# Two graph layers fused in one loop: announced jumps back, moved reads and copies, and a new order of small steps on VectorE

## The chip, the cores and the metric

One core of a Trainium2 chip runs the whole program. The metric is the device time of one execution in microseconds (us), lower is better. The engines are TensorE (PE, with its weight loads PEld), VectorE (DVE), ScalarE (ACT), GpSimd (POOL) and SyncE (SP); a small q behind a name (DVEq) is that engine's sequencer, which reads registers, waits for semaphores and issues.

## The reference, cut to what matters

There are 6250 nodes with 256 features and 206250 edges, sorted by target node. Layer 1 sums, over a node's edges, the neighbour's features beside 64 edge features, multiplies by a message matrix, and passes the result through a layer norm, a three-layer perceptron and a second norm. Layer 2 computes for every edge a logit from 128 other edge features, and for every node a softmax over its edges of the neighbours' hidden rows.

```python
agg = segment_sum(concat(x[src], edge64) @ W_message, dst)
h = layer_norm(relu(agg) + x); x1 = layernorm(x + layer_norm(x + mlp(h)))      # layer 1
edge_h = lrelu(edge128 @ ew_W + ew_b); hid = lrelu(x1 @ w_W + w_b)              # layer 2
e = concat(hid[tgt], hid[nbr], edge_h) @ a_W + a_b
out = lrelu(segment_sum(softmax_over_tgt(e) * hid[nbr], tgt)); y = layernorm(x1 + out)
```

## The kernel before, in words

A preparing stage counts edges by block of 128 nodes and writes small tables. Then comes the fused stage, the subject here, and behind it the second gather stage, which lies from about 2985 us of the span to the end and which the diff does not touch.

The fused stage is one loop of 51 passes, written out on each engine by itself (`Fori` on SP, POOL, PE, ACT and DVE); the engines keep in step by counting semaphores alone. A pass p holds 32 positions kk, and on PE, ACT and DVE a hand-written order puts small steps of three jobs at these positions:

- **Edge logits.** At every kk PE multiplies one tile of 128 edges (`edge` on PE, L657) into one of five PSUM banks that ACT filled with the bias before (`seed`, L801, three positions ahead), and DVE reduces it to one logit column (`edge` on DVE, L1034). Banks go round, so a seed waits until DVE has read the bank's last tile, and PE waits for the seed. SP loads the edge features four tiles at a time into two halves (`feats`, L600).
- **Sorting the logits.** The logits of pass p-1 are split into three bf16 parts (`split_logits`, L1014 to L1019, five instructions), multiplied by a one-hot of the target's block (`tag_logits`, L1024, at kk 0 to 2), and `sort` on PE (L696, from kk 4) puts them in order. `tag_keys` (L1006) does the same to the keys, `slots` (L995) makes the one-hot of the places, `key_pairs` (L999) doubles the keys, `place` (L1030) copies the addresses at which POOL writes the sorted rows (L617).
- **Layer 1.** POOL gathers the neighbours' rows, 35 indirect DMAs a pass (`gathers`, L624), from indices that `pick` (L1041, eight a pass) copied out. `one_hot` (L1060) on DVE and `add_rows` on PE (L672) sum them into one bank, `take_sums` (L1068, kk 30) takes the sum, and a chain of node steps turns the block before into its result: on DVE `add_x` at 5, `first_norm` 7, `residual` 12, 15 and 18, `out_sum` 21, `out_norm` 23, `last_norm` 25 (L1128), `table` 30 (L1134 to L1140); on PE the matmuls between them (L731 for the perceptron, `turn_x1` at 28, `hidden` at 30, L751); on ACT the copies, and `take_p` at 31 (L848), which waits for the table.

Each engine carries out its own order in sequence; a wait holds everything behind it on that engine. On DVE a step that needs the result of the step just before waits for it with `wait_alone` (L111 to L114). `edges_at` (L565) and `tile_at` (L562) read a pass's numbers from a table in SBUF into registers; on DVE both stand at the head of the pass, before `split_logits`:

```python
with dve.Fori(0, n) as p:
    e = edges_at(dve, p)
    tile = tile_at(dve, p + 1)
    body(p, e, tile)
```

On SP a pass begins with `load_x`, which waits for `last_norm` of the pass before (L591), and the two reads; only then come the loads of the edge features.

Of the kernel before, what the change touches and what calls it, by code (L numbers as in the profile page):

```python
# [27 lines left out]
P = 128  # L28
# [30 lines left out]
def build(nc, a, n_nodes, n_edges):  # L59
# [24 lines left out]
    with ExitStack() as top:  # L84
# [30 lines left out]

# [341 lines left out]
        with ExitStack() as ctx:  # L458
# [108 lines left out]
            @block.sync  # L567
            def _(sp):
                def load(dst, src):
                    sp.dma_start(dst, src).then_inc(w_in, 16)  # L570

                load(w_edge[:, 0:D], a["ew_W"])
                for n, name in enumerate(("a_tgt", "a_nbr", "a_edge")):
                    load(row[name], a["a_W"][n:n + 1, :].to_broadcast([P, D]))
                for name in ("w_b", "ew_b", "aggr_scale", "aggr_bias", "out_scale", "out_bias"):
                    load(row[name], a[name].to_broadcast([P, D]))
                load(ab_col[:], a["a_b"].to_broadcast([P, 1]))
                for c in range(KC):
                    load(w_msg[:, c, :], a["W_message"][c * P:(c + 1) * P, :])
                    load(w_node[:, c, :], a["w_W"][c * P:(c + 1) * P, :])  # L580
                    for n in range(3):
                        load(w_mlp[:, n, c, :], a[f"mlp_W{n}"][c * P:(c + 1) * P, :])
                load(w_msg[0:DE0, KC, :], a["W_message"][D:D + DE0, :])
                for n in range(3):
                    load(b_mlp[:, n, :], a[f"mlp_b{n}"])

                def load_x(p):

                    sp.wait_ge(nx["x1"], p)
                    d = block_at(sp, p)  # L590
                    sp.dma_start(x_blk[:], a["x"][bass.ds(d * P, P), :]).then_inc(nx["x"], 16)  # L591

                n = count_of(sp)
                with sp.Fori(0, n) as p:
                    load_x(p)
                    e = edges_at(sp, p)
                    t0 = tile_at(sp, p)
                    for c in range(TILES // EB):
                        sp.wait_ge(o["y_ready"], p * TILES + (c * EB - EB + Y0))
                        sp.dma_start(feats[:, c % 2 * EB * P:(c % 2 + 1) * EB * P],  # L600
                                     a["edge128"][:, bass.ds(e * (TILES * P) + c * EB * P, EB * P)]).then_inc(f_in[c % 2], 16)
                        j, at = c, STARTS[c]
                        sp.wait_ge(o["summed"], p * NB_SUMS + (j + 1))
                        sp.dma_start(rows[:, at:at + SUMS[j], D:W0], a["edge64"][:, bass.ds(t0 + at, SUMS[j]), :]).then_inc(e_in[j], 16)
                load_x(n)
                wait_alone(sp, (nx["tab_out"], n * 16 + 16))
# [4 lines left out]
            def _(pool):  # L611
# [20 lines left out]
                with pool.Fori(0, n) as p:  # L632
# [11 lines left out]
            def _(pe):  # L644
# [130 lines left out]
                with pe.Fori(0, n) as p:  # L775
                    body(p)
# [14 lines left out]
            def _(act):  # L791
# [11 lines left out]
                def keep_triangle(p):  # L803
                    act.wait_ge(o["tri_ready"], p + 1)
                    act.wait_ge(o["turned"], p * U + 1)
                    s.copy(starts[:].rearrange("p u b -> p (u b)"), TRI).then_inc(o["tri_kept"], 1)

# [52 lines left out]
                def body(p):  # L860
                    for kk in range(TILES):
                        seed(p, kk + AHEAD)
                        if kk in (8, 16):
                            pack(p, (8, 16).index(kk))
# [10 lines left out]
                for kk in range(AHEAD):  # L875
                    seed(0, kk)
                n = count_of(act)
                with act.Fori(0, n) as p:
                    body(p)
                steps = [node[kk] for kk in sorted(node)]  # L880
# [14 lines left out]
            def _(dve):  # L895
# [102 lines left out]
                def key_pairs(p, at):  # L998
                    v.tensor_copy(key_two[:], key[:, :, bass.ds(at, TILES)].unsqueeze(3).to_broadcast([P, 3, TILES, 2])  # L999
                                  ).then_inc(o["keys_ready"], 1)  # L1000

# [26 lines left out]
                def place(w, u, e):  # L1028
                    dve.wait_ge(rows_out, w * (U * 16) + (u + 1) * 16)
                    v.tensor_copy(at_now[u][:], at_all[:, bass.ds(e * U + u, 1)]).then_inc(o["at_ready"], 1)  # L1030

# [4 lines left out]

                def pick(p, j, tile):

                    if not isinstance(p, int):
                        dve.wait_ge(o["summed"], p * NB_SUMS + (j + 1))  # L1040
                    v.tensor_copy(picked[j][:, 0:SUMS[j]], src_i[:, bass.ds(tile + STARTS[j], SUMS[j])]).then_inc(o["picked_ready"], 1)  # L1041
# [104 lines left out]
                pick_at = {(SUM_KK[j + 1] + 1 if j + 1 < NB_SUMS else TILES - 1): j for j in range(NB_SUMS)}  # L1146
                hot_at = {SUM_KK[j - 2] + 1: j for j in range(2, NB_SUMS)}

                def body(p, e, tile):
                    at = e * TILES  # L1150
                    split_logits(p, at)
                    for kk in range(TILES):
                        edge(p, kk)
                        if kk < 3:
                            tag_logits(p, kk)
                        if kk == 3:
                            find(p, at)
# [6 lines left out]
                        if kk in (9, 13):  # L1164
                            place(p, (9, 13).index(kk), e)
                        if kk == 10:
                            key_pairs(p, at)
# [10 lines left out]
                        if kk in (18, 21, 23, 27):  # L1178
                            slots(p, (18, 21, 23, 27).index(kk))
                        if kk in (19, 25, 29):  # L1180
                            tag_keys(p, (19, 25, 29).index(kk))
                        if kk in hot_at:
                            one_hot(p, hot_at[kk])
                        if kk in pick_at:
                            pick(p + 1, pick_at[kk], tile)
                        if kk in node:
                            node[kk](p)
                        if kk == 24:
                            base_of(p + 1)
# [15 lines left out]
                for u in range(U):  # L1205
                    v.tensor_copy(at_now[u][:], dump[:]).then_inc(o["at_ready"], 1)
                tile = tile_at(dve, 0)
                for j in range(NB_SUMS):
                    pick(0, j, tile)
# [3 lines left out]
                one_hot(0, 1)  # L1213
                n = count_of(dve)
                with dve.Fori(0, n) as p:
                    e = edges_at(dve, p)
                    tile = tile_at(dve, p + 1)
                    count[0] = 0
                    body(p, e, tile)
                e = edges_at(dve, n)  # L1220
                split_logits(n, e * TILES)
                for m in range(3):
                    tag_logits(n, m)
                for u in range(U):
                    place(n, u, e)
# [608 lines left out]
```

## Time and profile before

| what | value |
|---|---|
| median of 3 runs | 5291.64 us (5288.85 to 5291.9) |
| the profiled execution, its own time | 5291.46 us |
| its span | 5289.7 us |
| fused stage, 48 passes in step | about 319 to 2777 us of the span |
| mean granted TensorE clock | 0.892 |

The profile is one execution; its busy shares are means over stages with different limits. A row of waits counts idle time of an engine and names what ended it. Times in timelines count from the start of the span.

### The profile page before, as it was taken

Reading aid. Unit: us, or ns where it says so; the run is one execution under the profiler, and the core shown is the slowest. Engines: PE = TensorE matmul, PEld = TensorE weight load, DVE = VectorE, ACT = ScalarE, POOL = GpSimd, SP = SyncE. Lnnn points to the kernel's source line nnn. Section 1 sums busy time; section 2 is a strip of 40 time slices with the busy share of each in tenths; the row PEclk is TensorE's granted clock in tenths of the full one; section 3 lists DMA queues with packets and bytes.
Section 4 is the critical chain, followed back from the end, with each engine's and each line's share of the span. In section 5 each row is a group of like instructions: output and inputs, shape, how many; then the busy total and the mean of one; then the engine's idle time right before and its main releaser. Section 6 shows DMA issues by size and latency. Waiting matters only on the chain. (4 is left out here: it accounts for less than half of the span.)

```text
span 5289.7 us, 86818 instructions
## 1 busy us (share of the span) xinstructions
PE 3902.5 (74%) x18662; PEld 2967.3 (56%) x18663; DVE 3563.6 (67%) x11443; ACT 1726.2 (33%) x5121; POOL 3584.2 (68%) x3655
## 2 busy tenths in 40 slices
PE   4498989898989898988887366666666666666661
PEld 3366666666666666666665255555555555555551
DVE  8778888888888888888786455555555555555554
ACT  0133333232323333333332133333333333333334
POOL 0377776777777777777773277777777777777772
PEclk9799999999999999999998688888888888888886
DMA  1356555555555555555556334344444334433343
GB/s 44 96 164 170 158 164 154 165 155 161 157 162 157 160 157 160 157 162 160 157 164 94 101 107 106 106 106 106 106 106 106 106 106 105 107 106 106 106 105 64
DMA packets 544286, 679.76 MB, mean 129 GB/s; under 512 B 340246, under 2 KB 376430, under 8 KB 543996
## 3 DMA queue, kind: packets, MB, share of 16 engines
q0 software_dynamic: 174144, 469.02, 32.6%
q1 hardware_dynamic: 355132, 196.63, 13.8%
q10 hardware_dynamic: 14976, 13.69, 0.8%
q8 instruction: 18, 0.29, 0.0%
q14 instruction: 16, 0.13, 0.0%
HBM read 650.32 MB, written 27.79 MB: 128 GB/s over the span
## 5 line engine op out<-in xcount | busy, mean ns | idle before, releaser
L624 POOL DMA_INDIRECT rows<-in_x,picked x1785 | 1799.1, 1008 | 724.1 <-issue 686.0
L1499 POOL DMA_INDIRECT room<-nodetab,nbr_idx x1736 | 1643.8, 947 | 562.4 <-issue 490.2
L672 PE MATMUL bank<-rows,hot 128*128 128x320 f32 x3570 | 1237.5, 446 | 25.7 <-DMA rows<-in_edge 19.7
L657 PE MATMUL bank<-w_edge,feats 128*128 128x258 f32 x3264 | 1050.6, 411 | 213.0 <-DMA feats<-in_edge 108.7
L801 ACT COPY bank<-b_edge 128x258 f32<-128x258 f32 x1635 | 602.7, 377 | 1460.6 <-DVE unused L1034 1442.9
L1529 PE MATMUL bank<-room,w 128*128 128x258 f32 x3472 | 1037.9, 462 | 51.2 <-ACT w L1575 50.7
L1561 ACT ACTIVATE w<-off,logit 128x128 f32<-128x128 bf16 x1736 | 534.0, 388 | 1361.0 <-DVE logit L1613 1361.0
L1529 PEld LDWEIGHTS bank<-room,w 128*128 128x128 f32 x3472 | 802.8, 238 | 244.4 <-ACT w L1575 95.0
L1520 PE MATMUL bank<-ident,w 128*128 128x128 f32 x1736 | 307.4, 330 | 777.2 <-ACT w L1561 777.2
L657 PEld LDWEIGHTS bank<-w_edge,feats 128*128 128x128 f32 x3264 | 578.7, 200 | 433.3 <-ACT bank L801 197.6
L1034 DVE SCALAR_TENSOR_TENSOR unused<-bank,a_relu 128x258 bf16<-128x258 f32 x1632 | 687.5, 421 | 199.2 <-PE bank L657 173.6
L672 PEld LDWEIGHTS bank<-rows,hot 128*128 128x128 f32 x3570 | 704.7, 198 | 179.9 <-issue 41.9
L1520 PEld LDWEIGHTS bank<-ident,w 128*128 128x128 f32 x1736 | 233.3, 166 | 824.0 <-ACT w L1561 437.0
L1618 DVE TENSOR_REDUCE best<-bank 128x1 f32<-128x896 f32 x248 | 270.7, 1091 | 475.0 <-PE bank L1520 474.9
L1613 DVE TENSOR_TENSOR logit<-r_at,room 128x7 f32<-128x7 f32 x248 | 42.4, 171 | 455.4 <-DMA room<-nodetab,nbr_idx 454.6
L1608 DVE TENSOR_SCALAR off<-iota_bf,lane_f 128x128 bf16<-128x128 bf16 x1736 | 337.8, 276 | 1.6 <-issue 1.6
L696 PE MATMUL bank<-tagged,slot 128*128 128x300 bf16 x1664 | 283.5, 293 | 54.9 <-DVE tagged L1024 54.6
L1637 DVE TENSOR_TENSOR w<-w,bank 128x896 f32<-128x896 f32 x248 | 268.5, 1083 | 58.2 <-PE bank L1512 55.3
L1060 DVE TENSOR_TENSOR hot<-iota,rel 128x512 f32<-128x512 f32 (+1 forms) x410 | 300.8, 734 | 0.1
L696 PEld LDWEIGHTS bank<-tagged,slot 128*128 128x128 bf16 x1664 | 159.4, 98 | 198.6 <-issue 143.0
L1575 ACT ACTIVATE w<-w 128x896 f32<-128x896 f32 x248 | 231.7, 934 | 4.4 <-DVE w L1637 4.4
L617 POOL DMA_INDIRECT recs<-out_rows,at_now x106 | 107.3, 1012 | 111.9 <-ACT out_rows L815 80.9
(316 smaller groups left out, 3871.4 us busy)
## 6 DMA issues: line engine op xcount, KB each, us to landing
feats<-in_edge SPq DMA_DIRECT2D x408, 256.0 KB, 2.9
rows<-in_edge SPq DMA_DIRECT2D x255, 128.0 KB, 3.0
rows<-in_x,picked POOLq DMA_INDIRECT x1785, 2.9
room<-nodetab,nbr_idx POOLq DMA_INDIRECT x1736
rows<-in_edge SPq DMA_DIRECT2D x153, 160.0 KB, 3.4
nodetab<-tab ACTq DMA_DIRECT2D x52, 129.0 KB, 2.7
x_blk<-in_x SPq DMA_DIRECT2D x52, 128.0 KB, 2.1
x_rows<-u_n ACTq DMA_DIRECT2D x52, 128.0 KB, 2.3
```

The lines of the kernel that those rows point to most:

```text
L624: pool.indirect_dma_start(out=rows[:, STARTS[j] + s, 0:D], out_offset=None, in_=a["x"], in_offset=bass.IndirectOffsetOnAxis(ap=picked[j][: ...
L657: mm(y, feats[:, f0 * P:(f0 + 1) * P], w_edge[:], start=False, stop=True, skip_group_check=True).then_inc(o["y_ready"], 1)
L672: ins = mm(S_PS, hot[j % HR][:, s - STARTS[j], :], rows[:, s, :], start=(s == 0), stop=(s == SA - 1), skip_group_check=True)
L696: ins = mm(SORT, slot[:, at, :], tagged[:, at, :, :, :].rearrange("p n f b -> p (n f b)"), start=(t == 0), stop=(t == L - 1), skip_group_c ...
L801: s.copy(logits_of(kk), b_edge[:]).then_inc(o["seeded"], 1)
L1034: v.scalar_tensor_tensor(unused[:, kk % EB, :], logits_of(kk), 0.0, a_relu[:], ALU.max, ALU.mult, accum_out=r_cur[:, kk:kk + 1]).then_inc( ...
L1060: v.tensor_tensor(hot[j % HR][:, 0:SUMS[j], :], iota[:].unsqueeze(1).to_broadcast(shape), rel[:, at:at + SUMS[j]].unsqueeze(2).to_broadcas ...
L1499: pool.indirect_dma_start(out=nbr[:, u * GC + k, :], out_offset=None, in_=nodetab, in_offset=bass.IndirectOffsetOnAxis(ap=nbr_idx[u][:, k: ...
L1520: ins = nc.tensor.transpose(T_PS[u % 2][:, k * P:(k + 1) * P], w[:, u * GC + k, :], ident[:])
L1529: ins = mm(O_PS[u % 2][:, 0:HW], w[:, u * GC + k, :], nbr[:, u * GC + k, :], start=(k == 0), stop=(k == GC - 1))
L1561: ins = s.activation(w[:, u * GC + k, :], off[:, u * GC + k, :], ACT.Identity, bias=logit[u][:, k:k + 1])
L1608: v.tensor_scalar(off[:, u * GC + k, :], iota_bf[:], lane_f[:, bass.ds(tile0(i, u) + k, 1)], MASKED, ALU.not_equal, ALU.mult)
```

## The change

On DVE `split_logits` moves from the head of a pass to the end of the pass before, `edges_at` is read at kk 0 and `tile_at` at kk 18. `place`, `key_pairs` and `pick` (eleven copies a pass) go from DVE to ACT, with reads of the same numbers there at kk 3 and 5. The steps `tag_keys`, `slots`, `base_of`, `local` and `one_hot` of the next pass get other positions.

```diff
+        def passes_of(eng, start, end):
+            return nc.Fori(start, end, engines=bass.OrderedEngineSet([eng.engine]), hint_back_edge=True)
...
-                with sp.Fori(0, n) as p:
-                    load_x(p)
+                with passes_of(sp, 0, n) as p:
...
+                        if c == 0:
+                            load_x(p)
...
                     for kk in range(TILES):        # ACT
                         seed(p, kk + AHEAD)
+                        if kk == 3:
+                            e = edges_at(act, p)
+                        if kk == 5:
+                            tile = tile_at(act, p + 1)
+                        if kk in (9, 13):
+                            place(p, (9, 13).index(kk), e)
+                        if kk == 6:
+                            key_pairs(p, e)
+                        if kk in pick_at:
+                            pick(p + 1, pick_at[kk], tile)
...
+                for u in range(U):                 # ACT, before its loop, after its first three seeds
+                    s.copy(at_now[u][:], dump[:]).then_inc(o["at_ready"], 1)
+                tile = tile_at(act, 0)
+                for j in range(NB_SUMS):
+                    pick(0, j, tile)
...
-                def body(p, e, tile):              # DVE
-                    at = e * TILES
-                    split_logits(p, at)
+                def body(p):
                     for kk in range(TILES):
                         edge(p, kk)
                         if kk < 3:
                             tag_logits(p, kk)
+                        if kk == 0:
+                            at = edges_at(dve, p) * TILES
+                        if kk == 18:
+                            tile = tile_at(dve, p + 1)
...
-                        if kk in (9, 13):
-                            place(p, (9, 13).index(kk), e)
-                        if kk == 10:
-                            key_pairs(p, at)
...
-                        if kk in (18, 21, 23, 27):
-                            slots(p, (18, 21, 23, 27).index(kk))
-                        if kk in (19, 25, 29):
-                            tag_keys(p, (19, 25, 29).index(kk))
+                        if kk in (18, 21, 26, 28):
+                            slots(p, (18, 21, 26, 28).index(kk))
+                        if kk in (17, 20, 25):
+                            tag_keys(p, (17, 20, 25).index(kk))
...
-                        if kk in pick_at:
-                            pick(p + 1, pick_at[kk], tile)
...
-                        if kk == 24:
+                        if kk == 22:
                             base_of(p + 1)
                             go_on(p)
-                        if kk == 25:
+                        if kk == 23:
                             local(p + 1, tile)
-                        if kk == 26:
+                        if kk == 24:
                             one_hot(p + 1, 0)
-                        if kk == 28:
+                        if kk == 27:
                             one_hot(p + 1, 1)
                         if kk == 30:
                             take_sums(p)
+                    split_logits(p + 1, at + TILES)
```

## Rows read from the trace of the kernel before

**Rows 1.** The page: busy us of each engine, its share of the span, instructions.

```profile
PE 3902.5 (74%) x18662; PEld 2967.3 (56%) x18663; DVE 3563.6 (67%) x11443; ACT 1726.2 (33%) x5121; POOL 3584.2 (68%) x3655
```

**Rows 2.** Windows: length, busy us of PE, PEld, DVE, ACT, POOL, clock, DMA share, GB/s.

```profile
319.20:2778.00 2458.80, 2213.65 (x10203) 1613.60 (x10202) 1986.86 (x6914) 758.36 (x2303) 1769.29 (x1756) 0.96 0.56 160
```

**Rows 3.** Waits in the same stretch: waiter, releaser, us in total, times, longest.

```profile
POOL rows L624 <- issue: 645.0, 1609, 4.0
...
PE bank L657 <- ACT bank L801: 101.3, 137, 2.1
PE bank L657 <- DMA feats<-in_edge: 91.6, 47, 3.0
...
DVE r_rest L1014 <- issue: 88.8, 48, 2.0
...
PE bank L696 <- DVE tagged L1024: 51.2, 42, 1.9
...
DVE h_t L1109 <- PE bank L731: 18.3, 47, 0.4
```

**Rows 4.** DVE's first step of a pass, L1014: ns min/median/max, first and last start.

```profile
L1014 DVE TENSOR_TENSOR r_rest<-r_cur x48: 191/193/194, 319.2 to 2777.2; 128x32 f32<-128x32 f32 x48
```

**Rows 5.** Timeline of one pass, layer 2 of the perceptron and kk 25.

```profile
2022.68 0.61 DVE L1109 SCALAR_TENSOR_TENSOR h_t<-bank,b_mlp,h_t 128x128 f32<-128x128 f32 x2 [0.39 <-PE bank L731]
...
2033.14 0.99 DVE L1006 TENSOR_TENSOR tagged<-hb,key_two 128x1600 bf16<-128x1600 bf16 x1
...
2034.04 0.16 DVE L1041 COPY picked<-src_i 128x4 int32 x1
...
2034.11 0.16 DVE L1085 RECIPROCAL rstd<-std 128x1 f32<-128x1 f32 x1
```

**Rows 6.** Timeline of the same pass's end and the next one's head.

```profile
2034.36 0.41 DVE L1128 TENSOR_SCALAR u_n<-u,mv,rstd 128x256 f32<-128x256 f32 x1
...
2037.54 1.12 PE L751 MATMUL bank<-w_node,h_t 128*128 128x256 f32 x4
...
2040.04 0.41 DVE L1134 TENSOR_TENSOR u<-bank,row_w_b 128x256 f32<-128x256 f32 x1
...
2042.97 0.29 ACT L848 ACTIVATE p_all<-p_cur,ab_col 128x1 f32 x1 [3.69 <-DVE stats L1140]
...
2043.80 2.09 PE L657 MATMUL bank<-w_edge,feats 128*128 128x258 f32 x4 [1.83 <-ACT bank L801]
...
2045.34 0.19 DVE L1014 TENSOR_TENSOR r_rest<-r_cur 128x32 f32<-128x32 f32 x1 [1.85 <-issue]
...
2046.21 0.43 DVE L1034 SCALAR_TENSOR_TENSOR unused<-bank,a_relu 128x258 bf16<-128x258 f32 x1 [0.19 <-DVE r_two L1019]
...
2050.28 0.68 PE L696 MATMUL bank<-tagged,slot 128*128 128x300 bf16 x4 [0.39 <-DVE tagged L1024]
```

**Rows 7.** DVE's jump and table read by line, 300 to 2800 us.

```profile
L1215 DVEq COMPARE_BRANCH  x48: 56/56/56, 316.9 to 2774.9; - x48
L1215 DVEq FUSED_REGOPS  x48: 74/74/74, 317.2 to 2775.2; - x48
...
L565 DVEq TENSOR_LOAD <-pass_tab x48: 521/531/689, 317.3 to 2775.3; - x48
```

**Rows 8.** DMA queues in 300 to 2800 us, all of them: packets, MB, share.

```profile
q0 software_dynamic: 85520, 225.99, 31.1%
q1 hardware_dynamic: 282056, 161.27, 23.9%
q10 hardware_dynamic: 13824, 12.64, 1.5%
```

**Rows 9.** The edge matmuls of the whole span, by line.

```profile
L657 PE MATMUL bank<-w_edge,feats x3264: 378/381/802, 207.4 to 2905.0; 128*128 128x258 f32 x192
```

**Rows 10.** Timeline of the start of the fused stage.

```profile
203.76 1.07 DVE L1041 COPY picked<-src_i 128x5 int32 x8 [0.84 <-issue]
...
206.62 1.67 ACT L801 COPY bank<-b_edge 128x258 f32<-128x258 f32 x5 [2.65 <-issue]
...
214.86 2.50 PE L672 MATMUL bank<-rows,hot 128*128 128x320 f32 x4 [5.49 <-DMA rows<-in_x,picked]
```

More of the change, by code:

```diff
@@ L631, in _ @@
                 n = count_of(pool)
-                with pool.Fori(0, n) as p:
+                with passes_of(pool, 0, n) as p:
                     gathers(p, 0)
@@ L774, in _ @@
                 n = count_of(pe)
-                with pe.Fori(0, n) as p:
+                with passes_of(pe, 0, n) as p:
                     body(p)
@@ L806, in keep_triangle, with place, key_pairs, pick @@
                     s.copy(starts[:].rearrange("p u b -> p (u b)"), TRI).then_inc(o["tri_kept"], 1)
+                def place(w, u, e):
+                    act.wait_ge(rows_out, w * (U * 16) + (u + 1) * 16)
+                    s.copy(at_now[u][:], at_all[:, bass.ds(e * U + u, 1)]).then_inc(o["at_ready"], 1)
+                def key_pairs(p, e):
+                    act.wait_ge(o["tagged_ready"], p + 1)
+                    s.copy(key_two[:], key[:, :, bass.ds(e * TILES, TILES)].unsqueeze(3).to_broadcast([P, 3, TILES, 2])
+                           ).then_inc(o["keys_ready"], 1)
+                def pick(p, j, tile):
+                    if not isinstance(p, int):
+                        act.wait_ge(o["summed"], p * NB_SUMS + (j + 1))
+                    s.copy(picked[j][:, 0:SUMS[j]], src_i[:, bass.ds(tile + STARTS[j], SUMS[j])]).then_inc(o["picked_ready"], 1)
+                SUM_KK = [SUM_AT[at] for at in STARTS]
+                pick_at = {(SUM_KK[j + 1] + 2 if j + 1 < NB_SUMS else TILES - 1): j for j in range(NB_SUMS)}
                 def pack(w, u):
@@ L876, in _ @@
                     seed(0, kk)
+                for u in range(U):
[3 more added lines that the diff above has]
+                    pick(0, j, tile)
                 n = count_of(act)
-                with act.Fori(0, n) as p:
+                with passes_of(act, 0, n) as p:
                     body(p)
+                e = edges_at(act, n)
+                for u in range(U):
+                    place(n, u, e)
                 steps = [node[kk] for kk in sorted(node)]
@@ L996, in slots @@
                                     ALU.is_equal).then_inc(o["slot_ready"], 1)
-                def key_pairs(p, at):
-                    v.tensor_copy(key_two[:], key[:, :, bass.ds(at, TILES)].unsqueeze(3).to_broadcast([P, 3, TILES, 2])
-                                  ).then_inc(o["keys_ready"], 1)
                 def tag_keys(p, n):
@@ L1026, in tag_logits @@
                         ins.then_inc(o["tagged_ready"], 1)
-                def place(w, u, e):
-                    dve.wait_ge(rows_out, w * (U * 16) + (u + 1) * 16)
-                    v.tensor_copy(at_now[u][:], at_all[:, bass.ds(e * U + u, 1)]).then_inc(o["at_ready"], 1)
                 def edge(p, kk):
@@ L1035, in edge @@
                                            accum_out=r_cur[:, kk:kk + 1]).then_inc(o["logit_ready"], 1)
[L1037 to L1041, printed above, removed]
                 def base_of(p):
@@ L1145, in _ @@
                 SUM_KK = [SUM_AT[s] for s in STARTS]
-                pick_at = {(SUM_KK[j + 1] + 1 if j + 1 < NB_SUMS else TILES - 1): j for j in range(NB_SUMS)}
                 hot_at = {SUM_KK[j - 2] + 1: j for j in range(2, NB_SUMS)}
-                def body(p, e, tile):
-                    at = e * TILES
-                    split_logits(p, at)
+                def body(p):
                     for kk in range(TILES):
@@ L1204, in _ @@
                 dve.sem_inc(nx["s"], 1)
-                for u in range(U):
-                    v.tensor_copy(at_now[u][:], dump[:]).then_inc(o["at_ready"], 1)
                 tile = tile_at(dve, 0)
-                for j in range(NB_SUMS):
-                    pick(0, j, tile)
                 base_of(0)
@@ L1213, in _ @@
                 one_hot(0, 1)
+                split_logits(0, 0)
                 n = count_of(dve)
-                with dve.Fori(0, n) as p:
-                    e = edges_at(dve, p)
-                    tile = tile_at(dve, p + 1)
+                with passes_of(dve, 0, n) as p:
                     count[0] = 0
-                    body(p, e, tile)
-                e = edges_at(dve, n)
-                split_logits(n, e * TILES)
+                    body(p)
                 for m in range(3):
                     tag_logits(n, m)
-                for u in range(U):
-                    place(n, u, e)
                 count[0] = 0
```

## The prediction, made before the changed kernel was run

> **What bounds the kernel now.** I read the page first: no engine is busy for more than three quarters of the span, so averages say nothing [rows 1]. The change touches only the fused stage, so I cut that out. Its passes are steady: 47 lie between the first and the last start of DVE's first step, 2458.0 us, or 52.30 us each [rows 4]. Per pass (the busy times over 47) PE is busy 47.1, DVE 42.3, POOL 37.6, ACT 16.1 us [rows 2]. POOL needs more than it shows: it leaves about 0.30 us between two of its 37 DMAs, so 37.6 + 11.1 = 48.7 us, and has 3.6 us of room a pass (its "issue" wait is 645.0/47 = 13.7 us, mostly those 0.30s) [rows 3]. That is a floor for later.
>
> Then the waits, to see who paces whom. DVE waits 0.39 us a pass for layer 2 of the perceptron (18.3/47), idles 1.85 us at the head of its pass on "issue", and PE waits for DVE's `tagged` 1.1 us, for ACT's seeds 2.2 us, for `feats` 1.9 us [rows 3]. The timeline orders this. From 2022.68, where DVE waits 0.39 us for layer 2 [rows 5], it never waits for PE again until after the pass's end: table at 2040.04, pass head at 2045.34, first edge at 2046.21. PE in turn runs dry there (1.83 us for a seed at 2043.80, 0.39 for `tagged` at 2050.28), and from `sort` at 2050.28 it is full until it hands layer 2 back to DVE [rows 6]. So a pass is two stretches in series: **DVE's** from layer 2 (kk 18) across the pass's end to `sort`, 2022.68 to 2050.28, 27.6 us; and **PE's** from `sort` to layer 2, the other 24.7 us. What shortens the first counts; what leaves DVE in the second does not, since DVE waits there for PE anyway.
>
> **Pass numbers read in mid-pass, logits split before the jump.** Of DVE's 1.85 us, the two reads are 2 x (0.53 + about 0.4 of register work) [rows 7]. In the new order edge 31 is followed by the split after a wait of about 0.19 us (what such a wait for its own result costs, [rows 6]), 0.68 us of split instructions, then jump and register work, about 0.55 us, then edge 0. Before, from the end of edge 31 to edge 0 it was 1.85 + 0.16 for the last `pick`, + 0.87 (2045.34 to 2046.21) = 2.8 us or so; now 0.19 + 0.68 + 0.55 = 1.4 to 1.5. **Gain 1.3 us** on DVE up to `tag_logits`. The reads themselves move under cover: at kk 0 behind a 0.99 us `tagged` product, at kk 18 behind `tag_keys` (0.99) and an edge (0.42) that are already issued; a read is about 0.9 us of sequencer. I take nothing, with 0 to 0.5 each if the queue is empty.
>
> How much passes through to `sort`? PE must be there too. It waits for `tagged` in 42 of 47 passes, 1.1 us on average, from 0 to 1.9 [rows 3]. The reason for the spread is PE's clock: the granted clock of this stretch is 0.96 on average [rows 2], and the four edge matmuls at 2043.80 take 2.09 us [rows 6], where the usual one takes 0.38 and the slowest 0.80 [rows 9]. After its dry spell PE works for a while at 1.2 instead of 2.4 GHz, now longer, now shorter. Of DVE's 1.3 us PE can use at most what it waited in each pass: with waits spread from 0 to 1.9 around 1.1 that is about **1.0 us**; bounds 0.4 (the pass shown) and 1.3.
>
> **Copies moved, steps reordered.** A `pick` is 0.16 us long but overlaps: 2034.04 to the next start 2034.11 is 0.07 us [rows 5]. Four of the eight stand in DVE's stretch before the table: 0.28 us. The others, both `place` and `key_pairs` stand in PE's stretch or are counted above: nothing. `tag_keys` 0 goes from kk 19 to 17, ahead of the wait for layer 2: DVE arrives 0.9 later (2033.14 to 2034.04) where it idled 0.39 and loses a 0.07 `pick`, so it saves 0.46. All the other moved steps stay between layer 2 and the table. Sum 0.74 us. What it opens: `last_norm` now has only 3.7 us of DVE work between itself and the table (three edges less two products; before 5.3, 2034.77 to 2040.04), and PE's `hidden` ends 3.9 us after it (2037.54 + 1.12) of which some was waiting for a seed that now comes sooner [rows 6]. So a new wait of 0 to 0.3 us; I take 0.15. **Gain 0.6 us**, bounds 0.1 and 0.8. The table lets ACT's `take_p` go (2042.97), and that the seed and PE at 2043.80, so this 0.6 moves both sides of the meeting at `sort` and passes through whole.
>
> On ACT eleven copies, at 0.29 (its 128x1 instruction [rows 6]) to 0.4, and two reads: about 4.5 us beside 16.1 busy of 52.3 [rows 2]. Their waits are for things long done (`summed` two positions back). If one blocked, the seeds behind it would wait, and PE for them.
>
> **SP.** Features for edges 0 to 3 leave earlier, so PE's 1.9 us for `feats` goes [rows 3]. But edges 2 and 3 still wait for the seed that hangs on the table: the idle time moves there. Nothing.
>
> **Start.** The first indices are now copied by ACT, behind PE's priming (206.62), three seeds, two copies and a read: first index about 208.8 instead of 203.8, and PE's first sum waits for those rows (5.49 us) [rows 10]. **+5 us**, once.
>
> **The sum.** 0.6 + 1.0 - 0.1 = 1.5 us a pass, times 48 passes in step (the first and the last two are paced by other things) = 72; less 5 = 67. Against the profiled execution, 5291.46 - 67 = 5224; that run stands 0.2 us from the median, so **5225 us**, -1.3%. Its own range: with 0.4 for the head, 0.9 a pass, 43 - 5, 5253; with 0.8 and 1.3 and nothing for the announcement, 2.1 a pass, 101 - 5, 5195.
>
> **Rivals.**
> 1. *The half-clock stretch decides.* If PE's slow spell begins as late and lasts as long with less waiting around it, PE's own 6 us from 2043.80 to 2050.28 set `sort` and only the table's 0.5 or so is left, or a read is exposed: 0.5 x 48 - 5 = 19, **5272**. For it: the pass shown gives DVE only 0.39. Against: 42 of 47 passes wait for `tagged`.
> 2. *More passes through.* The slow spell disappears as the dry spell shrinks, PE is always ready first, and DVE's whole 0.74 + 1.35 + a saved jump count: 2.2 x 48 = 106, no start cost, **5186**. POOL's room of 3.6 us a pass would allow it. Against: the seed still hangs on the table, so PE still runs dry.
> 3. *Slower: the announcement fetches.* If each announced jump brings in instructions that DVE or ACT then waits for, the price is a transfer's; the nearest rows are a DVE jump without one (0.25 us) and, far off, PE's longest wait for a landing, 3.0 us [rows 3]. At 2.1 us a pass, 101, against 67 saved: +34, **5326**. It decides from 1.4 us a pass. Against: nothing is fetched now, so what would be brought in is already there.
> 4. *The change does nothing*: PE's stretch grows by what DVE's loses, because ACT's added copies hold seeds up. 5290.
>
> The Trainium skill (Runtime: NRT & Kernel Launch, Instruction fetch mechanics) says that a taken branch whose target has left the sequencer's two-page window stalls on a fetch. By that rule, if DVE's long body outgrew the window, the jump's stall would be what the announcement removes. In this trace jump and queues show no such stall, so by the trace the term is nothing; the same rule stands beside rival 3, where code is fetched anew.
>
> **Chances.** Forecast 0.50, rival 1 0.17, rival 2 0.15, rival 3 (and ACT held up for longer) 0.10, rival 4 0.08. Within 0.2% (10.6 us), about what a measurement of this kernel can tell from no change, lies only rival 4: faster 0.82, same 0.08, slower 0.10. The range that leaves 2 in 10 out runs from rival 2's side to rival 1's: 5180 to 5280.
>
> **What would show it.** Starts of `split_logits` about 50.8 us apart; the "issue" idle at L1014 gone, with some 0.2 us after edge 31; POOL's "issue" wait down by 1.5 a pass; `feats` waits on PE gone and seed waits grown; `tagged` waits shrunk to a few tenths on average; granted clock about 0.96 as before; no instruction packets in 300 to 2700 us. Instruction packets in every pass, a new gap behind L1215 or L878, or ACT waits for L672 would make me wrong.

## The result and the profile after

The changed kernel takes **5194.64 us** (median of 4 runs, 5190.34 to 5199.08), the kernel before 5290.25 us beside it (4 runs, 5285.57 to 5291.9): ratio 0.9822, 95% interval 0.981 to 0.9833. That is 96 us less where 67 were forecast. It lies inside the range of 5180 to 5280, but 30 us below the forecast of 5225 and only 9 above rival 2's 5186. The profiled span is 5196.8 us, 92.9 less than before's.

Four views answer to those of before. The page, with each engine's busy us, share and instructions (before: [rows 1]):

```profile
PE 3824.1 (74%) x18662; PEld 2950.1 (57%) x18663; DVE 3511.6 (68%) x10870; ACT 1807.9 (35%) x5694; POOL 3555.6 (68%) x3655
```

573 instructions left DVE and as many came to ACT: the copies. Windows and waits of the fused stage, columns as in [rows 2] and [rows 3]:

```profile
319.20:2684.00 2364.80, 2133.19 (x10199) 1594.31 (x10199) 1939.85 (x6392) 832.26 (x2820) 1742.32 (x1757) 0.98 0.61 166
```

```profile
POOL rows L628 <- issue: 553.6, 1530, 3.7
...
PE bank L661 <- ACT bank L805: 200.6, 94, 2.8
DVE unused L1065 <- PE bank L661: 172.0, 315, 1.1
...
PE bank L700 <- DVE tagged L1059: 31.1, 21, 1.6
DVE u L1115 <- PE bank L722: 30.3, 47, 1.8
```

DVE's first step of a pass, `split_logits`, now L1049 ([rows 4]):

```profile
L1049 DVE TENSOR_TENSOR r_rest<-r_cur x48: 192/226/256, 319.6 to 2684.8; 128x32 f32<-128x32 f32 x48
```

47 passes take 2365.2 us, 50.32 each: 2.0 less than the 52.30 of [rows 4]. Beside it, compared with before: no wait for `feats` stands in the list any more, PE's wait for seeds has grown from 2.2 to 4.3 us a pass (200.6/47), its wait for `tagged` comes 21 times instead of 42, DVE's "issue" idle before the split is gone, POOL's "issue" has gone from 13.7 to 11.8 us a pass. All of these were forecast in kind. Two were off in size: the passes were to be 50.8 us apart, and the wait for `tagged` a few tenths of a us, where it is 31.1/47 = 0.66. Not forecast is the clock, 0.98 where it was 0.96 [rows 2]. PE's busy time shrank with it, 2213.65/47 = 47.1 to 45.4 us a pass, for the same matmuls.

The timeline of one pass's end (start, duration, idle before and its releaser; compare [rows 6]):

```profile
2027.62 0.42 DVE L1159 TENSOR_TENSOR u<-bank,row_w_b 128x256 f32<-128x256 f32 x1
...
2030.54 0.29 ACT L869 ACTIVATE p_all<-p_cur,ab_col 128x1 f32 x1 [2.66 <-DVE stats L1165]
...
2031.10 0.21 DVE L1049 TENSOR_TENSOR r_rest<-r_cur 128x32 f32<-128x32 f32 x1
...
2031.44 2.03 PE L661 MATMUL bank<-w_edge,feats 128*128 128x258 f32 x4 [2.80 <-ACT bank L805]
...
2032.50 0.43 DVE L1065 SCALAR_TENSOR_TENSOR unused<-bank,a_relu 128x258 bf16<-128x258 f32 x1 [0.60 <-DVE r_two L1054]
...
2032.85 0.99 DVE L1059 TENSOR_TENSOR tagged<-hb,r_two 128x1600 bf16<-128x1600 bf16 x1
...
2036.57 0.69 PE L700 MATMUL bank<-tagged,slot 128*128 128x300 bf16 x4
```

The table still lets the seed and the edge matmuls go 3.8 us later (2027.62 to 2031.44). But DVE's split starts 3.5 us after the table where it was 5.3, the first edge 4.9 where it was 6.2, and `sort` stands 8.95 us behind the table, with no wait, where it was 10.2 and waited.

To set the runs beside each other I worked out the same three distances in every trace, as means over 44 passes from the fourth on: from PE's first `sort` matmul to DVE's layer 2 residual, from there to the table's first step, and from there to the next `sort`. They add up to the pass. The last column is how many us of a pass PE's granted clock stood at the lower of its two levels, 1.2 instead of 2.4 GHz. All are us.

| kernel | sort to layer 2 | layer 2 to table | table to sort | pass | at half clock |
|---|---|---|---|---|---|
| before | 24.68 | 17.36 | 10.25 | 52.29 | 4.58 |
| after | 25.04 | 16.27 | 9.02 | 50.33 | 2.25 |
| announcement alone | 24.68 | 17.37 | 10.27 | 52.32 | 4.50 |
| head emptied alone | 24.68 | 17.35 | 9.19 | 51.21 | 5.20 |
| after, old positions | 24.95 | 16.91 | 9.34 | 51.19 | 4.96 |
| after, copies on DVE | 25.11 | 16.33 | 9.04 | 50.49 | 2.48 |
| after, no announcement | 25.05 | 16.25 | 8.96 | 50.26 | 2.48 |
| after, blocks first | 25.04 | 16.27 | 9.00 | 50.31 | 2.33 |
| after, reads at the head | 25.90 | 16.27 | 10.86 | 53.03 | 3.80 |
| one-hots early | 24.95 | 15.71 | 9.03 | 49.69 | 3.18 |
| seed before the table | 23.99 | 16.33 | 9.09 | 49.41 | 1.63 |

The last two rows are those of the two further steps at the end of the experiments. The traces also say which engine sets `sort`. In before it starts 0.24 us behind DVE's last `tagged` product in all of the 44 passes, and in after in 42 of them: DVE is the late one. DVE's own way, from the table to the end of that product, is 10.01 us in before and 8.73 in after.

### The profile page after: what moved, and what is told of

The parts are those of the page before. It is cut to its first block and busy times, and to the rows that moved or that the text cites. A ratio compares the mean times of both kernels' runs of the same rounds, so it can differ in the third digit from the quotient of the medians.

```text
span 5196.8 us, 87738 instructions
## 1 busy us (share of the span) xinstructions
PE 3824.1 (74%) x18662; PEld 2950.1 (57%) x18663; DVE 3511.6 (68%) x10870; ACT 1807.9 (35%) x5694; POOL 3555.6 (68%) x3655
## 5 line engine op out<-in xcount | busy, mean ns | idle before, releaser
L628 POOL DMA_INDIRECT rows<-in_x,picked x1785 | 1766.5, 990 | 660.0 <-issue 591.0
L661 PE MATMUL bank<-w_edge,feats 128*128 128x258 f32 x3264 | 999.7, 396 | 223.2 <-ACT bank L805 210.4
```

What stands on the lines that cost most here:

```text
L628: pool.indirect_dma_start(out=rows[:, STARTS[j] + s, 0:D], out_offset=None, in_=a["x"], in_offset=bass.IndirectOffsetOnAxis(ap=picked[j][: ...
L661: mm(y, feats[:, f0 * P:(f0 + 1) * P], w_edge[:], start=False, stop=True, skip_group_check=True).then_inc(o["y_ready"], 1)
```

## The experiments

### What the announcement does: dropped, and made alone

`e1_no_announce` is the changed kernel without the hint, in all five loops. `e6_announce_alone` is the kernel before with nothing but the hint.

```diff
 def passes_of(eng, start, end):
-    return nc.Fori(start, end, engines=bass.OrderedEngineSet([eng.engine]), hint_back_edge=True)
+    return nc.Fori(start, end, engines=bass.OrderedEngineSet([eng.engine]))
```

> The changed kernel with the announcements of the jumps alone taken out of all five loops. Main theory: nothing was fetched in the loops before, so the announcement is one instruction more on DVE and on ACT; without it the pass stays at 50.3 us or loses 0.1, so 5190 to 5196 us against 5194.6. Rival (the announcement brought a part of the gain that was not forecast, 0.4 us of the 1.96 a pass): pass 50.7 us, 5215 us or more.

> The kernel before with nothing but the announcements added to its five loops. Theory after the run without them: DVE's way from the table to the last tagged product gets 0.16 us longer, of which PE feels a part: pass 52.3 to 52.45, 5290 to 5300 us, never faster. Rival (the announcement pays where a loop's body is laid out differently): 5285 or less.

Measured: without it 5184.43 us (5183.77 to 5189.21, 5 runs), ratio to before 0.9801 (0.9788 to 0.9815), a little below what was expected; alone 5295.24 us, ratio 1.0002 (0.9993 to 1.0011). In the trace of after it is an instruction at the head of the pass (sequencer records of L1233: ns min/median/max, first and last start):

```profile
L1233 DVEq ALU_OP  x48: 40/40/40, 320.5 to 2685.7; - x48
L1233 DVEq COMPARE_BRANCH  x48: 61/61/61, 320.6 to 2685.8; - x48
L1233 DVEq BRANCH_PREFETCH_HINT  x48: 39/39/39, 320.9 to 2686.0; - x48
L1233 DVEq FUSED_REGOPS  x48: 62/63/63, 320.9 to 2686.1; - x48
```

From the start of DVE's branch to the first register record of the new pass it is 0.31 us, of which the announcement is one record of 0.04; in before it is 0.29 (316.9 to 317.2 in [rows 7]). So nothing is saved at the jump. Nor is anything fetched; these are all the DMA queues of 300 to 2700 us (packets, MB, share), while over the whole span two queues of kind "instruction" do show, with 33 packets:

```profile
q0 software_dynamic: 85496, 225.92, 33.8%
q1 hardware_dynamic: 281414, 160.96, 25.5%
q10 hardware_dynamic: 13824, 12.64, 1.5%
```

The Trainium skill (Runtime: NRT & Kernel Launch, Instruction fetch mechanics) has a jump pay for a fetch where its target has left the sequencer's window. By that rule the targets of these jumps would still be in it. The trace agrees: there are no instruction packets in either kernel, and a jump leaves about 0.25 us of idle time.

So rival 3 is out, and the price is about that of an instruction: 50.33 against 50.26 us a pass, 0.07 (0.1 charged), 3.4 us over 48 passes; made alone it is 52.32 against 52.29, 0.03. The medians of after and of this kernel lie 10 us apart, though the intervals of their ratios touch. Between the two traces 7.5 us are in the last pass of the loop (table to table 75.7 us in after, 68.2 here). That end isn't tied to the announcement: the kernel with reads at the head has it and took 68.3. What lengthens it stays open.

### The emptied head, alone

`e10_head_emptied_alone` takes the kernel before: split at the end of its own pass, both register reads under kk 0 and 1, steps and SP's order as before, no hint. The copies stay on DVE at their positions, but stand earlier within them.

```diff
-def body(p, e, tile):
-    at = e * TILES
-    split_logits(p, at)
+def body(p):
     for kk in range(TILES):
         edge(p, kk)
         ...
+        if kk == 0:
+            e = edges_at(dve, p)
+            at = e * TILES
+        if kk == 1:
+            tile = tile_at(dve, p + 1)
...
+    split_logits(p + 1, at + TILES)
```

> The kernel before with one part of the change: logits split at the end of their own pass, and the two reads under cover at kk 0 and kk 1. Copies stay on DVE, positions and SP's order are those of before, nothing is announced. Theory: DVE's way from table to the last tagged product is 1.4 us shorter (10.0 to 8.6), but PE's half-clock time stays at 4.6 us a pass or more, so PE sets sort and about 1.0 us passes through: pass 51.3, 5243 us. Rival (the head alone also frees the clock and all passes through): 50.9 or less, 5225.

Measured: 5239.39 us (5236.12 to 5241.11), ratio 0.9899 (0.9884 to 0.9914). Windows and waits of 400 to 2600 us:

```profile
400.00:2600.00 2200.00, 2025.82 (x9322) 1479.44 (x9321) 1812.36 (x6315) 692.14 (x2105) 1586.59 (x1601) 0.95 0.59 163
```

```profile
PE bank L699 <- DVE tagged L1040: 15.3, 15, 1.5
```

The pass is 1.08 us shorter, all of it between table and `sort` (10.25 to 9.19 us); the other two distances have not moved by more than 0.01. DVE's own way to the last `tagged` product fell by 1.45 us (10.01 to 8.56), where 1.3 were forecast; the rest is held back by PE. The waits for `tagged` fall to 0.35 us a pass, and in 26 of the 44 passes PE is the later of the two. These are the 26 in which it spends 6.8 us at half clock: table to `sort` takes 9.45 us in them, and 8.80 in the other 18, which have 3.4 us of it or none.

### The reordered steps, undone

`e4_old_positions` is the changed kernel with the tag, slot and index steps of DVE back where they were.

```diff
-if kk in (18, 21, 26, 28):
-    slots(p, (18, 21, 26, 28).index(kk))
-if kk in (17, 20, 25):
-    tag_keys(p, (17, 20, 25).index(kk))
+if kk in (18, 21, 23, 27):
+    slots(p, (18, 21, 23, 27).index(kk))
+if kk in (19, 25, 29):
+    tag_keys(p, (19, 25, 29).index(kk))
...
-if kk == 22:
+if kk == 24:
     base_of(p + 1)
     go_on(p)
-if kk == 23:
+if kk == 25:
     local(p + 1, tile)
-if kk == 24:
+if kk == 26:
     one_hot(p + 1, 0)
-if kk == 27:
+if kk == 28:
     one_hot(p + 1, 1)
```

> The changed kernel with slots, tag_keys, base_of, go_on, local and one_hot of the next pass at their positions of before. Main theory: tag_keys is again behind the wait for layer 2, so the stretch from layer 2 to the table is 0.8 us longer (16.3 to 17.1) and the stretch from sort to layer 2 0.36 shorter; net 0.4 to 0.5 a pass: 50.8 us, 5217. Rival (the order does nothing, the table is paced by PE's hidden): 5195.

Measured: 5235.38 us (5234.48 to 5239.64), ratio 0.9896 (0.9881 to 0.9911), 18 us above what was expected of it. Windows and waits of 400 to 2600 us, and the same pass end in its timeline:

```profile
400.00:2600.00 2200.00, 2010.46 (x9323) 1481.99 (x9322) 1775.04 (x5845) 750.97 (x2578) 1615.72 (x1603) 0.95 0.60 163
```

```profile
PE bank L661 <- ACT bank L805: 187.9, 128, 3.7
...
DVE slot L1034 <- issue: 28.2, 43, 0.7
```

```profile
2006.03 0.42 DVE L1159 TENSOR_TENSOR u<-bank,row_w_b 128x256 f32<-128x256 f32 x1
...
2009.51 0.19 DVE L1049 TENSOR_TENSOR r_rest<-r_cur 128x32 f32<-128x32 f32 x1
...
2009.86 1.14 PE L661 MATMUL bank<-w_edge,feats 128*128 128x258 f32 x4 [3.73 <-ACT bank L805]
```

The reordering is worth 0.86 us a pass here, of which 0.55 come before the table (24.95 + 16.91 against 25.04 + 16.27) and 0.32 between table and `sort`, where nothing was reordered. There PE is what differs: DVE's own way to the last `tagged` product is the same within 0.04 us (8.77 and 8.73). PE spends 4.96 us of a pass at half clock instead of 2.25 (0.95 and 0.98 on the windows rows), and the trace of e4 has the price in it: table to `sort` takes 9.71 us in the 21 passes with 6.8 us at half clock, and 9.00 in the 23 with 3.4 or less. In after only 2 of 44 passes have 6.8 us.

So it is the reordering that gave the better clock: neither the emptied head (e10, 0.95) nor, as the next run shows, the features. How it did so stays open. PE's dry spell before the seed is shorter, 2.80 us where e4 has 3.73, but its length alone does not explain the clock. The longest dry spell between table and `sort` is 2.1 us on average in before and 2.3 in e10, which have 4.58 and 5.20 us of half clock. With 2.8, as in after, the kernel with reads at the head has 3.80, and the one with early one-hots, at 2.7, has 3.18.

The second waits row holds a smaller surprise: the read at kk 18, free in after, shows as 0.66 us of "issue" before `slots` where no `tag_keys` stands ahead of it. DVE therefore comes to layer 2 too late to wait for PE, and `sort` to layer 2 is 24.95 us where before has 24.68. Some 0.27 of the 0.86 us are this exposed read, which before did not have. A second pair has no such read: the run with the copies on DVE against the emptied head alone, 50.49 against 51.21 us. It gives 0.72 us, of which 0.59 before the table, for the reordering together with the announcement and SP's order, which are worth -0.07 and nothing. The exposed read is also why e4 stands only 0.02 us below the emptied head alone (51.19 and 51.21), though it has the copies moved.

### SP's order undone

`e2_blocks_first` puts the load of the node block ahead of the feature loads again.

```diff
 with passes_of(sp, 0, n) as p:
+    load_x(p)
     e = edges_at(sp, p)
...
-        if c == 0:
-            load_x(p)
```

> The changed kernel with SP's load_x back at the head of a pass, so that the features of edges 0 to 3 leave late again. As forecast (the idle time of PE only moves to the seed): pass within 0.1 us of 50.3, total within 5 us of 5195. Rival (the one piece of idle instead of two is what halved the half-clock time, 4.6 to 2.25 us a pass): half-clock time back at about 4.5 us a pass, PE's way from edge 2 to sort 5.2 to 6.5 us again, pass 50.8 us or more, 5220.

Measured: 5196.06 us (5195.77 to 5200.51), ratio 0.9822 (0.9809 to 0.9836), and 50.31 us a pass. Waits of 400 to 2600 us:

```profile
PE bank L660 <- DMA feats<-in_edge: 118.8, 44, 3.2
...
PE bank L660 <- ACT bank L804: 64.5, 45, 1.5
```

The wait for `feats` is back, 2.7 us each time, and the seed's has shrunk from 4.3 us a pass by as much. PE idles the same time under another name, and its half clock is 2.33 us a pass, as good as in after. This edit is worth nothing, as forecast.

### The copies back on DVE

`e5b_copies_on_dve` gives DVE its `place`, `key_pairs` and `pick` again in the changed kernel, with its reads at kk 0 and 1; the first copies ahead of the loop are on DVE again too.

```diff
+if kk == 0:
+    e = edges_at(dve, p)
+    at = e * TILES
+if kk == 1:
+    tile = tile_at(dve, p + 1)
+if kk in (9, 13):
+    place(p, (9, 13).index(kk), e)
+if kk == 10:
+    key_pairs(p, at)
+if kk in pick_at:
+    pick(p + 1, pick_at[kk], tile)
```

> The changed kernel with place, key_pairs and pick back on DVE (and the first index copies with them), their two numbers read at kk 0 and kk 1. Theory: four picks of 0.07 us between layer 2 and the table, 0.3 us, the other seven copies under DVE's waits for PE: pass 50.6 us, 5205 us. Rival (a copy costs what its row shows, 1.9 us a pass, or ACT's relief of DVE is the main part of the gain): pass 51.3 or more, 5240.

> The same kernel as in e5_copies_on_dve, beside the kernel before at its usual time of about 5292 us. Theory: pass 50.6 us, 5205 us. Rival: pass 51.3 or more, 5240.

The first of the two ran on a chip where the kernel before itself took 6728.76 us (6699.69 for the experiment, ratio 0.9958); its times are not comparable with the rest. The same kernel is e5b, beside the kernel before at 5289.0 us. Measured there: 5194.77 us (5192.55 to 5200.28), ratio 0.9825 (0.9812 to 0.9839), the same as after. The pass is 0.16 us longer (50.49), 7.7 us in all, where 0.28 had been worked out. The first table stands at 260.1 us of the span against 265.8, and the loop's last pass takes 65.1 us instead of 75.7; that makes up for it, so the equal totals are in part chance. On ACT a copy costs less than I took (start, duration of two in a pass of after; 0.29 to 0.4 was the estimate):

```profile
2045.20 0.19 ACT L814 COPY at_now<-at_all 128x1 int32 x1
2045.29 0.19 ACT L824 COPY picked<-src_i 128x5 int32 x1
```

### The start

`e9_no_announce_first_picks` is e1 with the first indices copied by DVE ahead of its loop again.

```diff
-for u in range(U):
-    s.copy(at_now[u][:], dump[:]).then_inc(o["at_ready"], 1)
-tile = tile_at(act, 0)
-for j in range(NB_SUMS):
-    pick(0, j, tile)
...
+for u in range(U):
+    v.tensor_copy(at_now[u][:], dump[:]).then_inc(o["at_ready"], 1)
 tile = tile_at(dve, 0)
+for j in range(NB_SUMS):
+    v.tensor_copy(picked[j][:, 0:SUMS[j]], src_i[:, bass.ds(tile + STARTS[j], SUMS[j])]).then_inc(o["picked_ready"], 1)
```

> The changed kernel without the announcements and with the very first copies of indices (before the loops) on DVE again. Against the run without announcements, 5184 us, the first gather starts 5 us sooner and the first table with it: 5180 us.

The start of after, as it was forecast (compare [rows 10]):

```profile
208.96 0.86 ACT L824 COPY picked<-src_i 128x5 int32 x8
...
219.54 2.50 PE L676 MATMUL bank<-rows,hot 128*128 128x320 f32 x4 [5.96 <-DMA rows<-in_x,picked]
```

The first index stands at 208.96 us (208.8 forecast), PE's first sum 4.7 us and the first table 4.2 us later than before. Measured for e9: 5187.99 us (5187.46 to 5195.82), ratio 0.9808 (0.9795 to 0.9822), no better than e1, where 4 us less were expected. Its first table stands at 261.9 instead of 265.4 us, its last in the loop at 2801.3, as e1's (2801.4): the 3.5 us at the start are there and are lost again within the loop.

### The reads at the head

`e3_reads_at_head` leaves the split where after has it and puts the two register reads back at the head.

```diff
 def body(p):
+    at = edges_at(dve, p) * TILES
+    tile = tile_at(dve, p + 1)
     for kk in range(TILES):
         edge(p, kk)
...
-        if kk == 0:
-            at = edges_at(dve, p) * TILES
-        if kk == 18:
-            tile = tile_at(dve, p + 1)
```

> The changed kernel with DVE's two register reads back at the head of the pass; the split of the logits stays at the end. Main theory: 1.7 us of idle come back on DVE between the split and edge 0, tagged comes that much later, and since PE waits for it only 0.64 us on average today but is otherwise just in time, 1.4 to 1.7 us pass through: pass 51.9 us, 5270 us. Rival (PE's own way decides at sort): 0.5 us or less, 5220 or less.

Measured: 5322.45 us (5304.52 to 5326.69), ratio 1.0049 (1.0034 to 1.0065): slower than the kernel before, 52 us above what I expected. Windows and waits of 400 to 2600 us:

```profile
400.00:2600.00 2200.00, 1920.11 (x9021) 1421.16 (x9019) 1711.18 (x5643) 734.32 (x2488) 1555.91 (x1541) 0.96 0.58 157
```

```profile
DVE unused L1065 <- issue: 79.7, 32, 2.5
PE bank L700 <- DVE tagged L1059: 74.6, 41, 1.9
...
DVE u L1115 <- PE bank L722: 59.7, 41, 3.4
```

The head's "issue" idle is back at up to 2.5 us, now between the split and edge 0, so table to `sort` is 1.84 us longer. But PE's stretch from `sort` to layer 2 grew too, by 0.86 us, and this is all clock. In 30 of the 44 passes it takes 25.04 us, as in after. In the other 14 PE is at half clock for 5.3 to 5.8 us inside it, and it takes 27.65 to 27.85. DVE's wait for the message product rose with it, from 30.3/47 = 0.64 to 59.7/41 = 1.5 us a pass. What the expectation had left out is thus that idle time on DVE can bring PE more half clock, in a stretch that the edit does not touch.

### Two further steps from what the runs showed

`e11_hot_early` builds on e9. It makes six of the one-hot products earlier, into eight buffers instead of four.

```diff
-HR = 4
+HR = 8
...
-hot_at = {SUM_KK[j - 2] + 1: j for j in range(2, NB_SUMS)}
+hot_at = {4: 2, 8: 3, 10: 4, 12: 5, 13: 6, 14: 7}
```

> The kernel of the run just named, with eight buffers for the one-hots instead of four, so that the last three of a pass can be built at kk 12 to 14, where DVE waits for PE, and not at 16, 19 and 22. Nothing is taken away from DVE. Two-stretch theory: 1.4 us leave the stretch from layer 2 to the table and 0.3 of lateness at layer 2 goes; the pass falls by 1.5 us to 48.7, where POOL's 48.4 to 48.7 takes over: 5108 us (5095 to 5125). Rival (DVE's total work or PE paces the pass, not the stretch): within 15 us of 5180.

Measured: 5163.87 us (5161.17 to 5169.24), ratio 0.9757 (0.9744 to 0.977), 24 us below e9 where about 80 were expected. The stretch from layer 2 to the table is 0.57 us shorter (16.28 in e9, 15.71 here) where 1.4 were expected, and one thing came back, in 400 to 2600 us:

```profile
DVE slot L1029 <- issue: 18.7, 44, 0.4
```

With less queued ahead of it the read at kk 18 stands open for 0.42 us, and behind layer 2 DVE waits for an edge of PE, 0.73 us at 2035.31 of its timeline. The pass is 49.69 us, 0.57 less than e9's.

`e12b_seed_before_table` adds: that read at kk 21; the next seed issued on ACT ahead of `take_p`, so that PE has one more edge while it waits for the table; `take_sums` behind the table's first step; `sort` from kk 5.

```diff
 for kk in range(TILES):
-    seed(p, kk + AHEAD)
+    if kk > 0:
+        seed(p, kk + AHEAD)
+    if kk == TILES - 1:
+        seed(p, TILES + AHEAD)
...
-if kk == 18:
+if kk == 21:
     tile = tile_at(dve, p + 1)
...
-for u, first in enumerate((4, 12)):
+for u, first in enumerate((5, 12)):
```

> The kernel with the early one-hots, and PE's dry spell attacked: ACT fills the bank of edge 3 before it waits for the table, DVE takes the sums after the table's first step, sort starts at kk 5 instead of 4, and the read of the tile number stands at kk 21, behind a tagged product. Theory: PE's 2.75 us wait for the seed falls below 1 us, half-clock time falls with it, and PE is ahead by one position when tagged is ready; the pass falls from 49.7 to 48.7, where POOL's 48.4 to 48.7 stops it: 5118 us (5105 to 5145). Rival (DVE's way from table to tagged sets sort whatever PE does): 0.4 us from the read alone, 5145 to 5164.

> The same kernel as in e12_seed_before_table, beside the kernel before at its usual time of about 5292 us. Theory: PE's wait for the seed below 1 us, pass 48.7, 5118 us (5105 to 5145). Rival (DVE's way from table to tagged sets sort whatever PE does): 5145 to 5164.

The first ran on that same chip (6677.62 against 6728.76 us, ratio 0.9929), where its times cannot be compared with the rest. The same kernel beside the kernel before at 5289.0 us: **5151.59 us** (5147.97 to 5152.79), ratio 0.9738 (0.9725 to 0.9752), the fastest of all, but 34 us above what was expected and within the rival's range. Windows, waits and `split_logits`:

```profile
400.00:2600.00 2200.00, 2007.82 (x9641) 1495.78 (x9640) 1824.39 (x6064) 783.18 (x2668) 1690.73 (x1664) 0.98 0.62 170
```

```profile
POOL rows L628 <- issue: 453.0, 1479, 1.6
...
PE bank L661 <- ACT bank L805: 166.1, 90, 2.6
```

```profile
L1047 DVE TENSOR_TENSOR r_rest<-r_cur x48: 191/192/193, 315.8 to 2637.9; 128x32 f32<-128x32 f32 x48
```

PE's wait for the seed did not fall below 1 us: it is still up to 2.6. What stopped the gain is POOL. A pass is 2322.1/47 = 49.4 us. POOL is busy 1690.73/2200 of it, 38.0 us, and stands 0.31 us (453.0/1479) ahead of a DMA. With 37 or so of them that is 38.0 + 37.4 x 0.305 = 49.4, the whole pass. Of the 1664 gaps between its DMAs in this window only 3 are longer than 0.35 us, where after has 46 of them, which hold 1.9 us a pass beyond the 0.3. GpSimd is the bound of this stage now, at 0.7 us above the 48.7 that I had as its floor; as long as its DMAs stay as they are, there is next to nothing left to gain from DVE's or PE's order.

## Why the prediction was right, and which of its terms were not

The two stretches, the place of the gain and its order of size hold: 2.32 us left the stretch from layer 2 over the table to `sort` (27.61 to 25.29), where all of the 1.5 was put. By the steps of the sum, us a pass:

| step | forecast | measured | by |
|---|---|---|---|
| head: reads covered, split moved | 1.0 (0.4 to 1.3) | 1.08 | e10 against before |
| reordered steps, less a wait for `hidden` | 0.46 - 0.15 | 0.86 | after against e4 |
| copies to ACT | 0.28 | 0.16 | after against e5b |
| announcement | -0.1 (-0.25 to 0.25) | -0.07 | after against e1 |
| SP's order | 0 | 0 | after against e2 |
| sum | 1.5 | 2.03 | 1.96 in the pass |

The terms are not strictly additive: each is the difference of two traces, and the exposed read of e4 is in the second.

1.96 x 48 = 94; less 4.2 at the start (5 forecast), plus about 2 in the last two passes of the loop: 92, against 92.9 between the two spans.

- **The head** was right in working and share, a little small in both: DVE's way fell by 1.45 us where 1.3 stood in the sum, and 1.08 came through where 1.0 did. The reason for the share was right as well: in e10 PE is the later one in 26 of 44 passes.
- **The reordering is the step that was mis-sized**, 0.86 for 0.31 (0.72 by the pair without an exposed read). The gain before the table, 0.46 in the sum, was sound: 0.55 and 0.59 by the two pairs. Two things were off. The wait for `hidden` that I charged at 0.15 did not come. The matmul of `hidden` ends 0.28 us ahead of the table where it was 1.37: the margin was used up, not overdrawn. And the sum took the clock as given ("granted clock about 0.96 as before"). It rose to 0.98, PE's time at half clock fell from 4.58 to 2.25 us a pass, and the part of DVE's gain that I had left with PE came through. Rival 2 had this mechanism in part, against which I held that "the seed still hangs on the table, so PE still runs dry". That was true, and no reason: PE runs dry for 2.80 us in after and is still at half clock for half as long. What sets the time at half clock no run here shows. That 5195 fell between the forecast and rival 2 is therefore in part luck: the time at half clock could have risen as well as fallen, as it did in e10.
- **PE's stretch did not stay 24.7**: it is 25.04, since `tag_keys` 0 now stands ahead of layer 2 and DVE no longer waits there. Of the 1.09 us between layer 2 and table 0.36 were moved, not saved; net 0.73, which is the 0.74 of the forecast before its deduction.
- **The reads** are free only by what is queued ahead of them: nothing in after, 0.66 us in e4, 0.42 in e11. The bounds of 0 to 0.5 each were a little narrow.
- **Rival 1** (half clock decides) had the clock too strong: in e10 PE is at half clock the longest, 5.20 us, and 1.08 us still come through. It holds back 0.4 us of DVE's gain there, not most of it. **Rival 3** (fetches) has no instruction packet and no gap to show. **Rival 4** fell with the result: with the copies back on DVE neither PE's stretch nor the one from table to `sort` is shorter (25.11 and 9.04 against 25.04 and 9.02 us).

## What to carry to other kernels

Cut a pass at the points where the engines meet, and cost each edit on the stretch in which its engine is the late one; every term but one came out within 0.15 us so. Where the traced clock is below full in a stretch, do not carry it over as a constant: an edit on another engine can change it. Here that was worth a third of a microsecond a pass for the better, and with the reads at the head 0.86 for the worse. Put a range on it, and look at the passes one by one: those with more half clock show its price. A register read cost nothing behind a microsecond of queued work and about 0.9 us at the head of the loop, so its place is to be checked again whenever the steps ahead of it move.

## What the runs showed of the hardware

- PE's granted clock answered to the order of another engine's work, the matmuls being the same: 4.96 us of a pass at half clock in e4, 2.25 in after. The length of PE's longest dry spell does not order the kernels: 2.1 us goes with 4.58, 2.3 with 5.20, 2.8 with 2.25 and with 3.80, 3.7 with 4.96.
- 5.3 to 5.8 us at half clock inside PE's stretch from `sort` to layer 2 cost 2.6 to 2.8 us there (reads at the head).
- In these loops, in which no instructions are fetched, an announced jump back saves nothing (0.31 us from DVE's branch to the first register record, 0.29 without); the announcement is one record of 0.04 us and costs 0.03 to 0.07 us a pass.
- ScalarE copies 128x1 and 128x5 int32 in 0.19 us, where its 128x1 activation takes 0.29.
- GpSimd's indirect DMAs never came closer than 0.30 us after one another, and 37 of them with 38.0 us of busy time held the pass of the fastest kernel at 49.4 us.
